# A tuned two-layer recurrent kernel: three-pass attention output projection, attention's first projections among the last down products, no barrier between them

## The reference, cut to what matters

```python
x = L0_attn_x                                  # (2, 1024, 256)
xn = layernorm(x)
s = L0_attn(xn)       # 16 heads of 128, 4 kv heads, rope, elu+1 features, causal linear attention:
                      #   out = num / (den + 1e-6), then out @ Wo.T    (2048 -> 256)
g = silu(L0_ffn(xn))  # 8 experts of 176, top 2, plus a shared gated MLP: the gate, 256 wide
x = x + s * g
xn = layernorm(x)
s = L1_attn(xn)       # 32 heads of 64, state 64: decay = exp(-exp(xn @ w_dec)), z gate, norm, @ W_out.T
g = silu(L1_ffn(xn))  # int weights minus 128 with scales, 704 hidden units
x = x + s * g
```

## Time and profile before

| | |
|---|---|
| Time, median of 3 runs | 1776.44 us (the lowest 1776.33) |
| The profiled execution | 1777.31 us, of which its span 1775.5 us |
| TensorE (PE) busy | 1648.1 us, 93% |
| VectorE (DVE) busy | 1156.9 us, 65% |
| ScalarE (ACT) busy | 760.2 us, 43% |
| GpSimd (POOL) busy | 664.7 us, 37% |
| Mean granted TensorE clock | 0.971 of full speed |

### The profile page before, as it was taken

The page is one execution under the profiler, slowest core; times in us unless marked ns, Lnnn a source line. Parts: engine busy times, 40 slices in busy tenths (PEclk is TensorE's granted clock), DMA queues, the critical chain, the costliest instruction groups (busy, mean ns, idle before and its releaser), DMA issues.

```text
span 1775.5 us, 29643 instructions
## 1 busy us (share of the span) xinstructions
PE 1648.1 (93%) x11068; PEld 1366.1 (77%) x11068; DVE 1156.9 (65%) x2041; ACT 760.2 (43%) x1393; POOL 664.7 (37%) x500
## 2 busy tenths in 40 slices
PE   5997899898999999999869978998989999999988
PEld 3886677787878888887848857777978888888878
DVE  4333788663767788876743347886536677777767
ACT  4343445433434444444543334553334444444445
POOL 1453444200324444453514534441003244444535
PEclk9998999999999999999979989999999999999999
DMA  2333000000253344341023320000002533443410
GB/s 77 101 108 118 18 37 1 0 1 10 72 166 121 120 137 137 120 134 34 26 68 107 117 94 19 36 1 1 1 10 71 166 120 122 139 134 119 138 29 25
DMA packets 60061, 135.68 MB, mean 76 GB/s; under 512 B 8128, under 2 KB 12736, under 8 KB 59408
## 3 DMA queue, kind: packets, MB, share of 16 engines
q1 hardware_dynamic: 59920, 133.79, 23.6%
HBM read 130.81 MB, written 2.95 MB: 75 GB/s over the span
## 4 chain that ended last, share of the span: by engine, by line
PE 67%; DVE 11%; POOL 7%; issue 6%; ACT 5%; DMA 2%; SPq 0%; POOLq 0%; DVEq 0%; ACTq 0%
PE ps L553 31%; PE ps L610 6%; PE ps L872 4%; PE ps L896 4%; PE ps L649 4%; PE ps L834 3%; PE ps L589 3%; POOL silu_g L451 3%; PE ps L908 3%; POOL rb L469 2%; POOL fw_lo L436 2%; PE ps L883 2%; PE ps L751 2%; PE ps L752 2%; DVE hid L1347 2%
## 5 line engine op out<-in xcount | busy, mean ns | idle before, releaser
L553 PE MATMUL ps<-xnT_hi,w_in_hi 128*128 128x512 f32 x512 | 222.8, 435 | 0.0
L553 PE MATMUL ps<-xnT_lo,w_in_hi 128*128 128x512 f32 x512 | 203.6, 398 | 0.0
L553 PE MATMUL ps<-xnT_hi,w_in_lo 128*128 128x512 f32 x512 | 203.1, 397 | 0.0
L469 POOL TENSOR_TENSOR rb<-ra,rb 128x512 f32<-128x512 f32 x80 | 117.6, 1470 | 205.0 <-DVE rb L1537 205.0
L427 POOL TENSOR_TENSOR w_in_lo<-w_raw,w_in_hi 128x1024 fp32r<-128x1024 f32 x32 | 85.0, 2658 | 224.3 <-ACT w_in_hi L954 224.3
L1347 DVE TENSOR_TENSOR hid<-ps,silu_g 128x512 f32<-128x512 f32 (+1 forms) x80 | 55.1, 689 | 162.4 <-POOL silu_g L451 106.3
L1659 DVE TENSOR_TENSOR_SCAN lmat<-dec,ident 128x512 f32<-128x512 f32 x128 | 160.6, 1295 | 0.0
L516 POOL TENSOR_TENSOR yt<-yg,sz 128x512 f32<-128x512 f32 x64 | 83.5, 1305 | 155.4 <-ACT sz L1265 148.4
L553 PE MATMUL ps<-xnT_hi,fw_hi 128*128 128x512 f32 x312 | 126.7, 406 | 10.5 <-DVE fw_lo L1365 4.3
L436 POOL TENSOR_TENSOR fw_lo<-fw_raw,fw_hi 128x512 fp32r<-128x512 f32 (+1 forms) x56 | 62.7, 1121 | 185.3 <-ACT fw_hi L984 134.6
L1681 DVE TENSOR_TENSOR mt<-ps,lmat 128x512 f32<-128x512 f32 x128 | 82.5, 686 | 66.1 <-PE ps L872 66.1
(11 more groups left out here) (194 smaller groups left out, 4397.8 us busy)
## 6 DMA issues: line engine op xcount, KB each, us to landing
dec<-dec_dram SPq DMA_DIRECT2D x64, 512.0 KB, 4.0
w_raw<-in_w_in SPq DMA_DIRECT2D x32, 512.0 KB, 4.7
wdec<-dec_dram SPq DMA_DIRECT2D x128, 128.0 KB, 3.9
pdec<-dec_dram SPq DMA_DIRECT2D x128, 128.0 KB, 3.7
fw_raw<-in_fw SPq DMA_DIRECT2D x40, 384.0 KB, 3.1
w_raw<-in_w_qkv SPq DMA_DIRECT2D x8, 768.0 KB, 4.2
comb<-comb_dram SPq DMA_DIRECT2D x8, 512.0 KB, 3.7
w_out<-in_w_o SPq DMA_DIRECT2D x2, 2048.0 KB, 10.8
```

What stands on the lines that cost most here:

```text
L469: nc.gpsimd.tensor_tensor(rb[:, k], ra[:, k], rb[:, k], ALU.add).then_inc(a_rot.sem, 1)
L553: mm = nc.tensor.matmul(out, left(l, k), right(r, k), start=(j == 0), stop=(j == len(steps) - 1))
```

## The change

Three things change, in both batches.
- The output projection of attention works by half of the tokens and by head: 32 steps n, of which each has GpSimd multiply y of one head by 1/den (`normalised`, six of them while attention still runs), TensorE turn four tiles (`turn`) and make 12 three-pass matmuls (`project`), and ScalarE and VectorE split the turned y (`y_hi`, `y_low`). In the first 16 steps the weights are split as well (`w_hi_of`, `w_low`). Silu of the gate, eight pieces, is made by ScalarE in these first steps.
- The barrier between the gated layer and attention goes. TensorE makes attention's first projections between the last down products; the gate is copied to SBUF without silu; SP loads w_raw ahead of cos, sin and w_out; GpSimd splits w_raw between its last products.
- The barrier after the output projection goes. The second gated layer begins with the first half of the tokens of its tiles 0 and 1 (`FFN1_ORDER`), while the chunks 4 to 7 are still gated and normalised; the decay is made in two halves among them, in banks 6 and 7.

The diff, cut to its core (indented less; of the removed lines only the short ones are kept, the others are in the kernel above):

```diff
+def unit(b, k, hf):
+    u = 2 * (b * NF + k) + hf
+    return u + {(NF0, 1): 1, (NF0 + 1, 0): -1}.get((k, hf), 0)
+def before(b, k, hf):
+    return unit(b, k - 1, hf) if k > 0 else unit(b, k, hf) - 2
+def ffn1(x):
+    return NF0 + FFN1_ORDER[x][0], FFN1_ORDER[x][1]
+FFN1_ORDER = [(0, 0), (1, 0), (0, 1), (1, 1)] + [(k, hf) for k in range(2, NF1) for hf in range(2)]
...
+        def proj_bank(u, t):
+    return t if u % (2 * KVH) == 0 and t in (2, 3) else t % 2
...
-    sp.dma_start(cos[:], a["cos"]).then_inc(tables_in, 16)
-    sp.dma_start(sin[:], a["sin"]).then_inc(tables_in, 16)
-    sp.dma_start(w_out[:], a["w_o"]).then_inc(w_out_in, 16)
     for i in range(0, KVH):
+        if i == 1:
+            sp.dma_start(cos[:], a["cos"]).then_inc(tables_in, 16)
+            sp.dma_start(sin[:], a["sin"]).then_inc(tables_in, 16)
+            sp.dma_start(w_out[:], a["w_o"]).then_inc(w_out_in, 16)
...
             if k + 1 < NF0:
                 weights_lo(k + 1, hf)
+            else:
+                qkv_lo(0, hf)
+    qkv_lo(0, 2)
     nc.gpsimd.memset(v_tok[:, :, P:P + 1], 1.0)
-    for part in range(PARTS):
-        qkv_lo(0, part)
-    end_phase(pool, b, 1)
...
+    def normalised(n):
+        hf, t = n // NT - 2 * b, n % NT
+        pool.wait_ge(rin_step, 4 * b + (2 if t < (KVH - 1) * REP else 4))
+        part = y[:, 4 * hf:4 * hf + 4, t * P:(t + 1) * P]
+        nc.gpsimd.tensor_tensor(part, part, rin[:, 4 * hf:4 * hf + 4, t:t + 1].broadcast_to([P, 4, P]), ALU.mult).then_inc(o_yn.sem, 1)
+    for n in range(2 * b * NT, 2 * b * NT + EARLY_NORM):
+        normalised(n)
+    end_phase(pool, b, 1)
+    for n in range(2 * b * NT + EARLY_NORM, 2 * (b + 1) * NT):
+        normalised(n)
...
+    def turn(n):
+        hf, t = n // NT - 2 * b, n % NT
+        pe.wait_ge(o_yn.sem, o_yn.done(n))
+        pe.wait_ge(o_yl.sem, o_yl.done(n - 3))
+        for j in range(4):
+            mm = nc.tensor.transpose(ps[:, n % 3, j * P:(j + 1) * P], y[:, 4 * hf + j, t * P:(t + 1) * P], ident4[:, 0:P])
+        mm.then_inc(o_tr.sem, 1)
+    def project(n):
+        hf, t = n // NT - 2 * b, n % NT
+        if hf == 0:
+            pe.wait_ge(o_wh.sem, o_wh.done(b * NT + t))
+            pe.wait_ge(o_wl.sem, o_wl.done(b * NT + t))
+        pe.wait_ge(o_yh.sem, o_yh.done(n))
+        pe.wait_ge(o_yl.sem, o_yl.done(n))
+        for j in range(4):
+            for x, (l, r) in enumerate(SPLITS):
+                mm = nc.tensor.matmul(ps[:, 4 + 2 * hf + j // 2, (j % 2) * DM:(j % 2 + 1) * DM], yTs[l][:, n % YSLOTS, j * P:(j + 1) * P],
+                                      wa[r][:, t, :], start=(t == 0 and x == 0 and j % 2 == 0), stop=(t == NT - 1 and x == 2),
+                                      skip_group_check=True)
         mm.then_inc(o_mm.sem, 1)
+    n0 = 2 * b * NT
+    turn(n0)
+    turn(n0 + 1)
+    for n in range(n0, n0 + 2 * NT):
+        if n + 2 < n0 + 2 * NT:
+            turn(n + 2)
+        project(n)
+        t = n - n0 - NT
+        if t >= 0 and t % 3 == 2 and t // 3 < 4:
+            ln_transposes((b * 2 + 1) * NC + t // 3, t // 3 % 2, 3)
...
+    att_project(b * KVH, 0, 0, 0)
+    att_project(b * KVH, 0, 0, 1)
+    down(b, NF0 - 1, 0, False, True)
+    att_project(b * KVH, 0, 0, 2)
+    down(b, NF0 - 1, 1, False, True)
+    for t in range(3, REP + 2):
+        att_project(b * KVH, 0, 0, t)
     pe.wait_ge(a_clear, b + 1)
-    for t in range(REP + 2):
+    pe.wait_ge(f_gate.sem, f_gate.done(b * (4 + NC) + 3))
...
-    end_phase(pe, b, 3)
+    def decay(hf):
+        pe.wait_ge(o_sg.sem, o_sg.done(b * NC + 5 + 2 * hf))
+        pe.wait_ge(ln_hi.sem, ln_hi.done((b * 2 + 1) * NC + 4 * hf + 3))
+        pe.wait_ge(ln_lo.sem, ln_lo.done((b * 2 + 1) * NC + 4 * hf + 3))
+        return three_passes(ps[:, 6 + hf, :], lambda l, k: w_dec[l][:, k, :],
+                            lambda r, k: xnT[r][:, k, hf * HALF:(hf + 1) * HALF])
+    def ln_turned(c):
+        ln_transposes((b * 2 + 1) * NC + c, c % 2, 3)
+    pe.wait_ge(o_yl.sem, o_yl.done(2 * (b + 1) * NT - 1))
+    pe.wait_ge(ln_hi.sem, ln_hi.done((b * 2 + 1) * NC + 3))
+    pe.wait_ge(ln_lo.sem, ln_lo.done((b * 2 + 1) * NC + 3))
     gate_up(b, NF0, 0)
-    pe.wait_ge(s_dec.sem, s_dec.done(b))
-    gate_up(b, NF0, 1)
+    ln_turned(4)
+    decay(0)
+    ln_turned(5)
+    gate_up(b, NF0 + 1, 0)
+    ln_turned(6)
+    ln_turned(7)
+    decay(1).then_inc(s_loga.sem, 1)
+    gate_up(b, *ffn1(2))
+    for x in range(2 * NF1):
+        k, hf = FFN1_ORDER[x]
+        if x == 2:
+            gate_up(b, *ffn1(3))
+        if 2 <= x < 2 * NF1 - 2:
+            gate_up(b, *ffn1(x + 2), together=(FFN1_ORDER[x + 2][0] == NF1 - 1))
+        if x == 2:
+            pe.wait_ge(s_dec.sem, s_dec.done(b))
+        down(b, NF0 + k, hf, k == 0, k == NF1 - 1, rows=(64 if k == NF1 - 1 else P))
...
+    def w_hi_of(t):
+        if t == 0:
+            act.wait_ge(w_out_in, 16 * (2 * b + 1))
+        nc.scalar.activation(wa[0][:, t, :], w_out[:, t, :], ACT.Copy).then_inc(o_wh.sem, 1)
+    def y_hi(n):
+        act.wait_ge(o_tr.sem, o_tr.done(n))
+        act.wait_ge(o_mm.sem, o_mm.done(n - YSLOTS))
+        nc.scalar.activation(yTs[0][:, n % YSLOTS, :], ps[:, n % 3, :], ACT.Copy).then_inc(o_yh.sem, 1)
+    n0, n1 = 2 * b * NT, (b * 2 + 1) * NC
+    for n in range(n0, n0 + 2 * NT):
+        t = n - n0 - NT
+        if t < 0:
+            w_hi_of(n - n0)
+        y_hi(n)
+        if n - n0 < 2 * NC and (n - n0) % 2 == 1:
+            c = (n - n0) // 2
+            act.wait_ge(f_gate.sem, f_gate.done(b * (4 + NC) + c // 2))
+            nc.scalar.activation(gate[:, c, :], gate[:, c, :], ACT.Silu).then_inc(f_gate.sem, 1)
+        if 0 <= t < 12 and t % 3 == 0:
+            ln_std_of(n1 + t // 3, t // 3 % 2)
+        if 3 <= t < 15 and t % 3 == 0:
+            ln_hi_of(n1 + t // 3 - 1, t // 3 - 1, (t // 3 - 1) % 2, 3)
+        if t in (1, 2, 4, 5):
+            weights_hi1(b, *{1: (0, 0), 2: (0, 1), 4: (1, 0), 5: (1, 1)}[t])
+    for c in range(4, NC + 2):
+        if c == 7:
+            silu(b, NF0, 0, s_gu[:, 0, 0:1])
+        if c < NC:
+            ln_std_of(n1 + c, c % 2)
+        if c >= 6:
+            ln_hi_of(n1 + c - 2, c - 2, c % 2, 3)
...
+    def gate_copy(hf):
+        act.wait_ge(f_dn.sem, f_dn.done(unit(b, NF0 - 1, hf)))
         for x in range(2 * hf, 2 * hf + 2):
-            nc.scalar.activation(gate[:, 2 * x:2 * x + 2, :].rearrange("p c d -> p (c d)"), ps[:, 4 + x, :], ACT.Silu)
-    end_phase(act, b, 1)
+            nc.scalar.activation(gate[:, 2 * x:2 * x + 2, :].rearrange("p c d -> p (c d)"), ps[:, 4 + x, :],
+                                 ACT.Copy).then_inc(f_gate.sem, 1)
     def rope_act(n, hf, r):
...
             if kv_ahead:
                 rope_act(n + 1, hf, 0)
                 v_copy(n + 1, hf)
+    v_copy(b * KVH, 0)
+    gate_copy(0)
     rope_act(b * KVH, 0, 0)
-    v_copy(b * KVH, 0)
+    gate_copy(1)
...
+    def w_low(t):
+        dve.wait_ge(o_wh.sem, o_wh.done(b * NT + t))
+        nc.vector.tensor_tensor(wa[1][:, t, :], w_out[:, t, :], wa[0][:, t, :], ALU.subtract).then_inc(o_wl.sem, 1)
+    def y_low(n):
+        dve.wait_ge(o_yh.sem, o_yh.done(n))
+        dve.wait_ge(o_mm.sem, o_mm.done(n - YSLOTS))
+        nc.vector.tensor_tensor(yTs[1][:, n % YSLOTS, :], ps[:, n % 3, :], yTs[0][:, n % YSLOTS, :], ALU.subtract).then_inc(o_yl.sem, 1)
+    def add_gated(c):
         n = b * NC + c
+        dve.wait_ge(o_mm.sem, o_mm.done((2 * b + c // 4) * NT + NT - 1))
         dve.wait_ge(o_res.sem, o_res.done(n - 2))
+        dve.wait_ge(f_gate.sem, f_gate.done(b * (4 + NC) + 4 + c))
+        nc.vector.tensor_tensor(sg[:, c % 2], ps[:, 4 + c // 2, (c % 2) * DM:(c % 2 + 1) * DM], chunk(gate, c), ALU.mult).then_inc(o_sg.sem, 1)
         dve.wait_ge(o_sg.sem, o_sg.done(n))
+        nc.vector.tensor_tensor(chunk(x_res, c), sg[:, c % 2], chunk(x_res, c), ALU.add).then_inc(o_res.sem, 1)
+        dve.wait_ge(o_res.sem, o_res.done(n))
+        ln_stats(n1 + c, c, c % 2, n1 + c - 2)
+        ln_variance(n1 + c, c % 2, n1 + c - 2)
+    def normal(c):
+        ln_root(n1 + c, c % 2)
+        ln_norm(n1 + c, c, c % 2, c % 2)
+    n0, n1 = 2 * b * NT, (b * 2 + 1) * NC
+    for n in range(n0, n0 + 2 * NT):
+        t = n - n0 - NT
+        if t < 0:
+            w_low(n - n0)
+        y_low(n)
+        if 0 <= t < 12 and t % 3 == 0:
+            add_gated(t // 3)
+        if 0 <= t < 12 and t % 3 == 1:
+            normal(t // 3)
+        if 3 <= t < 15 and t % 3 == 0:
+            ln_low(n1 + t // 3 - 1, t // 3 - 1, (t // 3 - 1) % 2, 3)
+        if t in (2, 5, 8, 11):
+            weights_lo1(b, *{2: (0, 0), 5: (0, 1), 8: (1, 0), 11: (1, 1)}[t])
+    add_gated(4)
+    add_gated(5)
+    normal(4)
+    add_gated(6)
+    normal(5)
+    ln_low(n1 + 4, 4, 0, 3)
+    hidden(b, NF0, 0, f_silu, unit(b, NF0, 0))
+    add_gated(7)
+    normal(6)
+    ln_low(n1 + 5, 5, 1, 3)
+    normal(7)
+    ln_low(n1 + 6, 6, 0, 3)
+    ln_low(n1 + 7, 7, 1, 3)
```

273 lines of the change are left out of this document (94 added, 179 removed).

## The result

The changed kernel takes 1747.59 us (median of 4 runs, 1747.12 to 1750.44), the kernel before 1776.44 (1776.33 to 1780.14): 0.9835, 95% interval 0.9815 to 0.9856, or 1.65% faster, less than the 2% from which the prediction calls a kernel faster. A fourth run of the kernel before took 4640 us and is left out. The prediction was 1747.0 in 1728 to 1766. The profiled execution has a span of 1745.9 against 1775.5, 29.6 us less.

What follows compares the result with a forecast made beforehand. TensorE, busy for 93% of the span, was taken to bound the kernel: less work or closed gaps. Terms of -13.2, -7.1 and +5.6 sum to -14.7 us a batch, -29.4 in all, from 1776.4 to 1747.0, range 1728 to 1766.

Steps and rivals of the forecast that it cites:

- Term A: Seam into attention, up to the first score: earlier w_raw, earlier projections and no barrier save 13.2 us a batch.
- The price put on a missing cover: Seam into attention: 3.6 us given back if the silu of unit 26 still comes late.
- Term B: Output projection of attention: three-pass matmuls and no wait at its start save 7.1 us a batch, bounds 11.1 and 3.
- the bound of TensorE alone: Output projection: the gain if only TensorE sets its pace, 11.1 us a batch.
- the wait at step 17: Start of the projection's second half: y_low(17) comes late, 3.9 us against 2.3 that TensorE allows.
- the second half: Projection after half 0: VectorE needs 6.5 us per three-step group against TensorE's 5.9, so it takes 34.4 us.
- Term C: Projection's end to the state-space layer: waits and table loads make it 5.6 us a batch longer, bounds 0 and 9.
- the tail of the sum: After gate_up(1,1) starts: 1.5 us last wait, 1.5 late weights, two half-clock spells of 1.55 each.
- Rival 1: Whole kernel: VectorE keeps up in the projection's second half and the seam after it costs 0; 1728 us, chance 0.28.
- Rival 2: Seam into attention: an event that does not move binds the rotation chain, saving only 5 us; 1763 us, chance 0.14.
- Rival 3: Projection: gaps between steps bring the lower clock; 1807 us with half of it at 1.2 GHz, chance 0.06.

Runs made afterwards that it cites:

- e6: The changed kernel with SP's loads of cos, sin and w_out ahead of the first w_raw again, as before the change: 1752.8 us.
- e7: The changed kernel with both last down products of the gated layer again ahead of attention's projections 0, 1 and 2, still without barrier: 1751.4 us.
- e12: The changed kernel with the multiplication by 1/den moved from GpSimd back to VectorE: 1753.7 us.
- e2: The changed kernel with ScalarE's load and two exponentials of the decay moved from behind hidden_hi(1,0) to behind the silu of unit (0,1): 1736.6 us.
- e1: The changed kernel without the second normalisation's eight square roots on ScalarE; VectorE takes the reciprocal of the variance, so the output is not the reference's: 1736.9 us.
- e3: The changed kernel with unit (0,1) taken earlier on ScalarE, VectorE and TensorE, so that the decay's table load and exponentials lie behind it: 1735.8 us.
- e4: The kernel of e3 with the first part of the next weights split one unit earlier from tile 3 on: 1726.9 us.
- e5: The changed kernel with the second gated layer's hidden units in the plain order (0,0), (0,1), (1,0), (1,1) on every engine: 1727.8 us.
- e9: The kernel of e4 with silu and product of unit (0,0) earlier and VectorE's three instructions starting the decay's prefix one unit later: 1717.5 us.
- e11: The kernel of e5 with the first decay product made four times instead of once, where TensorE otherwise waits for chunk 6: 1724.9 us.

## Why the prediction was right, and where it was not

**Term A held, and its steps too**: w_raw's wait gone, the times within 0.2 us, -13.1 and -14.0 against -13.2. e6 and e7 show that both parts were needed. The price put on a missing cover was 3.6; in e6 the wait is 3.61, and the first score comes 4.0 later in batch 0 and 4.6 in batch 1.

**Term B was right in its mechanism and 3.5 us a batch too small.** From the barrier (343.0) to the end (406.14) it takes 63.1 where it took 73.7 from 354.5: -10.6, near the bound of TensorE alone. Step 0 came 2.2 after the barrier (forecast 2.4), half 0 ended 31.8 after it (32.2), GpSimd took 1.16 instead of 1.28, the wait at step 17 was 0.98 (1.6). The step that failed is the second half, 34.4 us: it took 31.3. The 34.4 were TensorE's 30.3, 1.6 for step 17 and four groups at 6.5 us of VectorE against 5.9 of TensorE; step 17 cost 0.98 and the groups nothing. I had 5.5 of work and 1.0 of waiting in a group; VectorE's second group (385.71 to 391.74) is 5.0 of work and 1.06 of waiting, and no instruction in it is locked, since GpSimd was done at 372.3, before that half began. The 0.2 that is left over TensorE's 5.83 I take to be absorbed by the three slots of yTs; no run here varies them. e12 shows what such a group does when VectorE really has more work than TensorE: the waits that I forecast appear.

From the score to the barrier lies another 1.7 us that the change didn't make: in one batch of each kernel a stretch of 13 us ran at 0.87 (batch 1 before, batch 0 after). That is why B reads -9.0 and -12.9.

**Term C had the right places and was too small: 5.6 for 12.2 and 7.1.** With 0 at the projection's end, gate_up(1,0) waited from 6.05 to 8.53 (forecast 6.3 to 8.9), decay(1) came at 14.7 (13.4), down(1,0) at 22.3 (20.95), gate_up(1,1) at 27.6 behind a wait of 3.31 (26.0, 3.6). From there to the state-space start it took 47.6 where the prediction has 42.4. The step that failed is the tail of the sum, 1.5 for the last wait, 1.5 for late weights and 1.55 for each of two spells at the lower clock. The waits there were 4.6 where 3.0 stood, and the lower clock cost 6.1 where 3.1 stood. I take the price of the clock as half of the time in which TensorE was busy at 0.50. Over the whole seam of batch 0 that is 8.1 us (half of 3.42, 6.93, 5.50 and 0.44 at the seam's end) against 1.7 before; in batch 1 it is 6.3 against 5.9. The waits are 5.9 and 6.1 more. Together that is 12.3 of the 12.2 in batch 0 and 6.5 of the 7.1 in batch 1. So what I mis-sized in both batches are the waits; the clock makes the difference between the batches, and the kernel before lost as much to it in batch 1.

The cause given for the waits, ScalarE's queue with its loads and exponentials, is shown by e2 (one move, 5.3 of its 11.0 us) and by e1 for the roots with their loads; e3 and e4 add the weights, which are late on VectorE. That the interleaving as written is what costs is shown by e5. Why the slow matmuls fall where they do stays open. I had the term's sign from the walk, and still didn't ask what the plain order would give.

**Rival 1** (everything kept, 1728) is not what happened, but e5 and e4 land on it, 1727.8 and 1726.9: the gain forecast there was in reach and was lost in the seam. **Rival 2** (an unmoved event in A) fell with the score at 175.20. **Rival 3** (a lower clock in the projection) did not occur: 1.00 throughout. The lower clock came in the seam instead (0.86), where I had given it 3.1 us.

## What to carry to other kernels

When work is interleaved on TensorE to fill a gap, walk the other engines' queues in the same order: here one table load with two exponentials ahead of a silu, and a weight split one unit late, turned the filler into a loss of 10 us a batch (5.5 of them waits). Moving them made the same interleaving as fast as the plain order (e4), and two more moves made it the fastest kernel (e9). Give the clock a range of its own in the sum: seams with the same waits differed by up to 4.6 us in it, as much as the terms under study. And a covered wait often shows up at the next event under another name (e3), so move on until the matmuls join up.

## What the runs showed of the hardware

Needless matmuls in a gap shortened the run (e11: 4.2 us of work more a batch, 3.0 us less in the median). In batch 0 the granted clock behind the gap stayed at 1.00 where it had been 0.50 and 0.63.

A table load need not wait for what its activation waits for: in e5 it starts at 418.27, right behind the instruction before, and the exponential starts at 421.19 when its matmul ends, so this load cost nothing. It isn't always so: in the kernel before, the load at 436.76 stood behind a wait of 5.10 for that product. Where ScalarE is busy, a switch costs the load and no more: one silu starts at 413.11, 1.30 us after its load at 411.81, itself right behind the activation before. The Trainium skill (ScalarE: Activation LUTs, section "What ACT_TABLE_LOAD costs") gives 1283 ns for the load, which agrees, and a drain of about 1.38 us on top of it, which none of these rows shows.

The multiplication of 128x512 by 1/den took 1.16 us on GpSimd and 0.68 on VectorE, and moving it to the faster engine made the kernel slower.
